# Graph network: the ranks of empty nodes and free slots move from the ordering stage into layer 0, with a weight split

## The reference

```python
edge_index = jnp.stack([src, dst])
h = jnp.maximum(_layernorm(x), 0.0)
x = x + _L0_gnn_ref(h, edge_index, L0_W1, L0_b1, L0_W2, L0_b2)
...
def gnn_layer(x, W, b, src, dst):          # _L0_gnn_ref: two of these
    h = x @ W.T + b
    agg = segment_sum(h[src], dst, num_segments=10000)
    return relu(agg)
```

## Time and profile before

| | us |
|---|---|
| median of 3 runs (2781.2 to 2782.97) | 2782.51 |
| the profiled execution | 2777.66 |
| its span in the profile | 2775.9 |
| Orders, from the first instruction after the barrier to that after the next | 290.0 to 342.9 |
| layer 0, first half | 342.9 to 668.8 |

### The profile page before, as it was taken

How to read it: one execution, slowest core, us unless ns; L and a number is a source line. 1 busy time by engine, 2 the same in 40 slices (tenths; PEclk the granted TensorE clock), 3 DMA queues, 4 the chain that set the end, 5 groups by cost and what they waited for, 6 DMA issues and landing times. The chain is left out here.

```text
span 2775.9 us, 48023 instructions
## 1 busy us (share of the span) xinstructions
PE 2503.1 (90%) x13886; PEld 2134.6 (77%) x13886; DVE 2015.0 (73%) x5259; ACT 1397.0 (50%) x2905; POOL 1739.8 (63%) x1849
## 2 busy tenths in 40 slices
PE   3666199998999969999999979999999699999998
PEld 3444088887888859999999868888888588888886
DVE  7888566664666637878788768888888566666666
ACT  0766054544888845555555434333333255555554
POOL 0777255554677776777777567777777455555554
PEclk9999999999999989999999989999999899999999
DMA  8888434333455543343333244333333255555553
GB/s 253 244 245 240 147 101 136 112 120 114 134 158 169 176 158 99 116 130 115 115 115 115 70 120 143 116 115 115 113 113 113 90 143 153 153 153 153 153 150 115
DMA packets 146046, 388.08 MB, mean 140 GB/s; under 512 B 34372, under 2 KB 34692, under 8 KB 145315
## 3 DMA queue, kind: packets, MB, share of 16 engines
q0 software_dynamic: 101408, 304.38, 37.0%
q1 hardware_dynamic: 43442, 80.04, 9.4%
q10 hardware_dynamic: 1056, 2.10, 0.2%
HBM read 261.83 MB, written 149.12 MB: 148 GB/s over the span
## 5 line engine op out<-in xcount | busy, mean ns | idle before, releaser
L1609 PE MATMUL c_pu<-c_Zhi,parts 128*128 128x256 f32 x640 | 182.1, 285 | 5.3 <-DVE c_Zlo L1527 5.3
L845 POOL DMA_INDIRECT f_Gsrc<-rows,indexS x80 | 80.5, 1006 | 168.6 <-PE f_phsrc L2110 159.7
L2026 ACT ACTIVATE f_Mhi<-f_pm 128x512 fp32r<-128x512 f32 x80 | 47.9, 599 | 266.1 <-DVE f_pm L2059 259.5
L1611 PE MATMUL c_pu<-c_Zhi,parts 128*128 128x256 f32 x640 | 181.6, 284 | 0.0
L1610 PE MATMUL c_pu<-c_Zlo,parts 128*128 128x256 f32 x640 | 180.5, 282 | 0.0
L2050 DVE TENSOR_TENSOR f_Hlosrc<-f_phsrc,f_Hhisrc 128x512 fp32r<-128x512 f32 x80 | 55.4, 692 | 158.6 <-ACT f_Hhisrc L2020 158.6
L1768 ACT CAST d_Hhi<-d_ph 128x512 fp32r<-128x512 f32 x80 | 46.8, 585 | 229.5 <-PE d_ph L1889 229.5
L849 POOL DMA_INDIRECT h<-a_rows,indexD x80 | 80.5, 1006 | 126.3 <-ACT a_rows L1184 119.7
L1496 ACT ACTIVATE c_pu<-c_pu,c_b1col 128x256 f32<-128x256 f32 x160 | 61.8, 450 | 162.6 <-PE c_pu L1611 162.6
L824 PE MATMUL b_po<-parts,b_Thi 128*128 128x512 f32 x320 | 132.6, 414 | 1.8 <-ACT b_po L1176 1.7
L824 PE MATMUL a_po<-parts,a_Thi 128*128 128x512 f32 x320 | 132.5, 414 | 0.4 <-DVE a_Tlo L1216 0.3
(11 more groups left out here) (461 smaller groups left out, 9623.0 us busy)
## 6 DMA issues: line engine op xcount, KB each, us to landing
rows<-r_xt SPq DMA_DIRECT2D x40, 520.0 KB, 4.0
h<-q_zerorow SPq DMA_DIRECT2D x80, 256.0 KB
r_xt<-in_x SPq DMA_DIRECT2D x80, 256.0 KB, 4.8
selrowsD<-selD SPq DMA_DIRECT2D x1, 2640.0 KB, 9.5
selrowsS<-selS SPq DMA_DIRECT2D x1, 2640.0 KB, 14.7
q_keyrowD<-in_dst POOLq DMA_DIRECT2D x1, 2560.0 KB, 17.7
q_keyrowS<-in_src POOLq DMA_DIRECT2D x1, 2560.0 KB
o_wstage<-in_L_W ACTq DMA_DIRECT2D x2, 1024.0 KB, 5.5
```

The source lines that it names most:

```text
L845: return pool.indirect_dma_start(out, None, table, bass.IndirectOffsetOnAxis(ap=rows, axis=0))
L1609: pe.matmul(psum_u[:, o, :], g.Whi[2][:, c, cols], Zhi[:, c, :], start=c == 0, stop=False)
L1611: ins = pe.matmul(psum_u[:, o, :], g.Wlo[2][:, c, cols], Zhi[:, c, :], start=False, stop=c == C - 1)
L2026: nc.scalar.activation(Mhi[s][:, :], psum_m[s][:, :], ACT.Relu).then_inc(s_Mhi, 1)
```

## The change

- Orders loads only one weight, `L0_W1`, on SP's queue and behind the wait for the records. ACT copies it in four quarters, and DVE instead of POOL subtracts, in four quarters, behind the step that makes `free`. `L0_W2` becomes the first of three weights that layer 0's first half loads and splits between its groups.
- SP writes `selrow` of D, waits for it, issues D's broadcast, and then does the same for S.
- The ranks leave Orders. That of empty nodes ("z") is worked out at the start of layer 0's first half, by PE and DVE before their loops; DVE's wait for the bias row stands behind it. That of free slots ("q") is cut up: PE has a piece behind groups 0, 2 and 4, DVE behind groups 1, 3 and 5. SP stores `qhi16` behind the third weight's load and waits for it before it issues the broadcast of `qdram`.
- PE's and DVE's loops have 6 groups written out in place of 2; ACT's are all written out. Some tiles have other places in memory.

```diff
@@ Orders, DVE
-                for m, (rows, out_row, name) in enumerate(((empty, zrow, "z"), (free, qrow, "q"))):
...
-                step(dve.tensor_copy(qhi16[:, :], qi[:, :]), "qhi16")
+                for c in range(C):
+                    dve.wait_ge(o_high, c + 1)
+                    dve.tensor_tensor(g.Wlo[0][:, c, :], wstage[:, c, :], g.Whi[0][:, c, :].bitcast(F32), ALU.subtract)
@@ Orders, ACT
-                for m in range(2):
-                    W.load_one(act, m)
-                    W.split_high(act, m)
+                act.wait_ge(o_w, 16)
+                for c in range(C):
+                    nc.scalar.copy(g.Whi[0][:, c, :], wstage[:, c, :]).then_inc(o_high, 1)
@@ Orders, POOL
-                for m in range(2):
-                    W.split_low(pool, m)
@@ Orders, SP
                 for k in KEYS:
                     sp.wait_ge(o_ld[k], 48)
-                for m, k in enumerate(KEYS):
+                sp.dma_start(wstage[:, :, :], io.L0_W1.rearrange("(c p) n -> p c n", p=P)).then_inc(o_w, 16)
+                for k in KEYS:
                     sp.wait_ge(o_v, marks["sel" + k])
                     sp.dma_start(g.seldram[k], selrow[k][:, :]).then_inc(o_sel[k], 16)
-                for k in KEYS:
                     sp.wait_ge(o_sel[k], 16)
                     sp.dma_start(g.selrows[k][:, :, :], g.seldram[k].partition_broadcast(P)).then_inc(o_bc[k], 16)
...
-                sp.wait_ge(o_v, marks["qhi16"])
-                sp.dma_start(g.qdram, qhi16[:, :]).then_inc(o_q, 16)
-                sp.wait_ge(o_q, 3 * 16)
+                sp.wait_ge(o_q, 2 * 16)
@@ layer 0, first half
-        W = None if second else Weights(nc, e, g, [(2, io.L1_W1), (3, io.L1_W2)])
+        W = None if second else Weights(nc, e, g, [(1, io.L0_W2), (2, io.L1_W1), (3, io.L1_W2)])
@@ SP
                 W.load(sp)
+                sp.wait_ge(n_step, marks["qhi16"])
+                sp.dma_start(g.qdram, qhi16[:, :]).then_inc(n_q, 16)
+                sp.wait_ge(n_q, 16)
                 sp.dma_start(qrow16[:, :], g.qdram.rearrange("t j -> (t j)").partition_broadcast(NT)).then_inc(e_ld, 16)
@@ ACT
-                pipeline(act, GR, 1, 1, body, between=lambda i: W.high_part(act, i), first=2 * C + 2)
+                straight(GR, 1, 1, body, between=lambda i: W.high_part(act, i))
@@ DVE
+            def step_node(ins):
+                ins.then_inc(n_step, 1)
+                steps[0] += 1
+                dve.wait_ge(n_step, steps[0])
+            def count_nodes(name, rows, m):
+                dve.wait_ge(n_pe, 3 * m + 1)
+                step_node(dve.tensor_copy(colform[:, :], pflag[:, 0:NT]))
+                if name == "z":
+                    step_node(dve.tensor_copy(emptyc[:, :], colform[:, :]))
+                step_node(dve.tensor_reduce(total[:, :], rows[:, :], AX.X, ALU.add))
+                step_node(dve.tensor_scalar(totals[:, :], g.ones_f[0:NT, :], total[:, 0:1], None, ALU.mult))
+            def place_nodes(name, m):          # 1 step, after a wait for PE
...
+            def split_ranks(name, m):          # 8 steps for z, 10 for q, after a wait for PE
...
+            def rank_free(i):
+                if i == 1:
+                    count_nodes("q", g.free, 1)
+                elif i == 3:
+                    place_nodes("q", 1)
+                elif i == 5:
+                    split_ranks("q", 1)
...
-            if not second:
-                dve.wait_ge(s_brow, 16)
             dve.wait_ge(s_const, 4 if second else 3)
...
-                pipeline(dve, GR, 1, 1, body)
+                count_nodes("z", g.empty, 0)
+                place_nodes("z", 0)
+                split_ranks("z", 0)
+                dve.wait_ge(s_brow, 16)
+                pipeline(dve, GR, 1, 1, body, between=rank_free, first=6)
@@ PE
+            def flag_nodes(name, rows, m):
+                if m:
+                    pe.wait_ge(n_step, marks["colz"])
+                pe.transpose(pflag[:, 0:NT], rows[:, :], g.ident[0:NT, 0:NT]).then_inc(n_pe, 1)
+            def count_up(name):                # 2 products
...
+            def turn_places(name):             # 1 transpose
...
+            def rank_free(i):                  # i == 0: flag, 2: count_up, 4: turn_places, of "q"
...
-                pipeline(pe, GR, 1, 0, body)
+                flag_nodes("z", g.empty, 0)
+                count_up("z")
+                turn_places("z")
+                pipeline(pe, GR, 1, 0, body, between=rank_free, first=6)
```

More of the change, by code:

```diff
@@ L131, in prepare_orders @@
     g.xs = [nc.dram_tensor(f"rows{n}", [N + 1, EXT], F32, kind="Internal").ap() for n in range(1, 4)]
+    g.hold = ExitStack()
+    held = Env(nc, g.hold, "h_")
+    g.empty, g.free = g.listed, held.sb("free", [NT, P], F32)
+    g.before_f, g.ones_f = held.sb("beforef", [P, P], F32), held.sb("onesf", [P, P], F32)
+    before_f, ones_f, empty, free = g.before_f, g.ones_f, g.empty, g.free
     with ExitStack() as ctx:
@@ L534, in prepare_orders @@
         tmp_c2 = sb("tmpc2", [P, NT], F32)
[L535 to L543, removed]
         with ExitStack() as c4:
@@ L712, in _ @@
                     pe.transpose(ptr[k][:, 2 * NT:3 * NT], length[k][:, :], g.ident[0:NT, 0:NT]).then_inc(o_pe, 1)
[L713 to L720, removed]
-                    pe.wait_ge(o_v, marks["row" + name])
-                    pe.transpose(prank[:, 0:NT], out_row[:, :], g.ident[0:NT, 0:NT]).then_inc(o_pe, 1)
             @block.sync
@@ L1007, in layer0 @@
     if not second:
-        g.hold = ExitStack()
-        g.qrow16 = g.hold.enter_context(nc.sbuf_tensor("qrow16", [NT, N], I16))
+        g.hold2 = ExitStack()
+        g.qrow16 = g.hold2.enter_context(nc.sbuf_tensor("qrow16", [NT, N], I16))
     qrow16 = g.qrow16
@@ L1040, in layer0 @@
             e_made, e_put, e_ld = e.sem("e_made"), e.sem("e_put"), e.sem("e_ld")
+            colform, total, totals = e.sb("colform", [P, NT], F32), e.sb("total", [NT, 1], F32), e.sb("totals", [NT, P], F32)
+            place = {k: e.sb("place" + k, [NT, P], F32) for k in "zq"}
+            rank_c = {k: e.sb("rankc" + k, [P, NT], F32) for k in "zq"}
+            whole, part_i, emptyc = e.sb("whole", [P, NT], I32), e.sb("parti", [P, NT], I32), e.sb("emptyc", [P, NT], F32)
+            qi, qhi16 = e.sb("qi", [NT, P], I32), e.sb("qhi16", [NT, P], I16)
+            pflag, psum_r, prank = (e.ps(n, [P, 512]) for n in ("pflag", "psumr", "prank"))
+            n_step, n_pe, n_q = e.sem("n_step"), e.sem("n_pe"), e.sem("n_q")
+            marks = {}
         s_brow, s_const = e.sem("s_brow"), e.sem("s_const")
@@ L1052, in layer0 @@
         block = ctx.enter_context(e.block())
+        if not second:
+            marks.update({"totalsz": 4, "placez": 5, "colz": 6, "totalsq": 16, "placeq": 17, "colq": 18, "qhi16": 27})
         @block.sync
@@ L1335, in put @@
                           stop=isinstance(T.t, int) and T.t == NT - 1).then_inc(e_put, 1)
+            def flag_nodes(name, rows, m):
[3 more added lines that the diff above has]
+            def count_up(name):
+                pe.wait_ge(n_step, marks["totals" + name])
+                pe.matmul(psum_r[0:NT, 0:P], colform[:, :], g.before_f[:, :], start=True, stop=False)
+                pe.matmul(psum_r[0:NT, 0:P], g.before_f[0:NT, 0:NT], totals[:, :], start=False, stop=True).then_inc(n_pe, 1)
+            def turn_places(name):
+                pe.wait_ge(n_step, marks["place" + name])
+                pe.transpose(prank[:, 0:NT], place[name][:, :], g.ident[0:NT, 0:NT]).then_inc(n_pe, 1)
+            def rank_free(i):
+                if i == 0:
+                    flag_nodes("q", g.free, 1)
+                elif i == 2:
+                    count_up("q")
+                elif i == 4:
+                    turn_places("q")
             def look(T):
```

56 lines of the change are left out of this document (28 added, 28 removed).

## The result

The changed kernel takes 2758.61 us (median of 6, 2757.4 to 2760.57); beside it the kernel before took 2782.05 (6, 2778.46 to 2782.97). The ratio is 0.9921, interval 0.9911 to 0.9932: faster by 23.4 us, where 17.8 was forecast. The profiled execution took 2758.56, its span is 2756.8, only 19.1 less than the profiled one of before.

The account below looks back on a forecast made before the run. Orders was taken to be bound by DVE's chain, layer 0's first half by PE. Orders' gain of 19.5 less 0.9 for z and 0.8 for q gave 17.8 us, so a median of 2764.7, range 2760.5 to 2772.

Parts of the forecast that it names:

- its whole 8.38: Orders: two long DVE steps beside POOL's subtractions become short, taking 8.38 us off DVE's chain.
- the 11.24: Orders: the stretch from 328.90 to 340.14 goes when the ranks leave, 11.24 us.
- The tables: Rival in Orders: S's table lands 5.4 us late and bounds in DVE's place; gain 12.7, time 2769.8; chance 0.15.
- the late case: Orders: S's store gets through only after D's broadcast; S's broadcast issued about 310.3, landing 319.8, 1 us to spare.
- Records: Start of Orders: loads ahead of the weight land in 2.4 us, DVE starts at 293.2; gain 2.9 us.
- I put the balance at 0: Layer 0's first half: third weight's transfer and qrow cost nothing on balance; bounds a gain of 1.6, a loss of 3.3.
- the bound of -1.6: Layer 0's first half: possible gain of 1.6 us if the pause before qrow lets the gathers through.
- its slow rival: Layer 0's loop: TensorE's lower clock lasting through groups 0 to 4 adds 77 us, time 2842; chance 0.03.
- I carry that difference over: Whole kernel: the profiled execution's 4.85 us below the median is kept, so 2759.9 profiled becomes 2764.7 median.
- the one that gained more than forecast: Rival: records land at 1.4 us and qrow's stall is gone; gain 20.3, time 2762.2; chance 0.12.
- the thin columns: Rival at Orders' start: thin columns take 5.1 us anyway, records not faster; gain 14.9, time 2767.6; chance 0.15.
- a costlier layer 0: Rival in layer 0: q at 2.1 us on PE and two transfer bursts; gain 13.2, time 2769.3; chance 0.10.

Follow-up runs that it names:

- e1: Kernel before with only the weight part changed: one weight in Orders, its subtraction on DVE, order of loads and ranks as before; 2774.77 us against 2780.0.
- e2: Changed kernel with both weights split in Orders by POOL and the old order of loads and stores, so only the ranks move; 2770.95 us, ratio 0.997.
- u1: Changed kernel with ACT issuing the weight's load at its start, beside the records' loads instead of behind them; 2763.36 us, ratio 0.9942 to the kernel before.
- b0: Kernel before, unchanged, profiled once more; 2780.99 us against 2780.0, its profiled execution 2780.75.
- a1: Changed kernel, unchanged, run once more beside the kernel before on one chip; 2757.1 us against 2781.47.
- u2: Changed kernel with the store of qdram ahead of the third weight, so weight and qrow follow at once; 2762.08 us, its profiled execution 2756.37.
- u4: Changed kernel with qdram's store ahead of the third weight, no pause before qrow, run a second time; 2759.09 us, ratio 0.9928 to the kernel before.
- p1: Kernel before with one wait added, for the second weight to land, ahead of qrow; 2776.6 us against 2780.3.
- w2: Changed kernel with 12 unused identity products ahead of PE's loop in layer 0's second half and 8 ahead of its first multiplication; 2756.39 us.
- v1: Changed kernel with DVE's four subtractions moved from Orders to layer 0's first half, the staged weight sharing memory; 2753.4 us, ratio 0.9904 to the kernel before.
- w1: Changed kernel with 12 unused identity products ahead of PE's loop in layer 0's second half; 2757.26 us, ratio 0.9915 to the kernel before.
- u3: Changed kernel with SP's old order, both selrow stores ahead of both broadcasts; 2758.49 us, ratio 0.9925 to the kernel before.

## Why the prediction missed, step by step

**Right.** Orders is DVE's chain, and what left the chain left the time. POOL's overlap was worth its whole 8.38 (e1, e2). The ranks were worth 7.95 and the 3.05 us that e2 waits, 11.0 of the 11.24. Orders of e1 and e2 with the 3.47 of u1 and those 3.05 give 5.95 + 7.95 + 3.47 + 3.05 = 20.4, and 20.6 to 20.8 were measured. The tables did not bind: by the reading of the Trainium skill, DMA: Bandwidth & Descriptors, section Queues, rings and completion order, S's store would sit behind D's broadcast. The trace agrees: D's broadcast lands at 300.70 + 8.7 = 309.4, S's store after 4.4 us at 309.6. S's broadcast was issued at 309.62, where the late case said 310.3. The clock of the loop stayed 1.00, and its regular tile 3.87 although more groups are written out.

**Small errors in Orders.** Records 3.4 to 3.5, not 2.9 (1.9 us to land, not 2.4); the subtraction 2.50, not 2.76; the tables 0, not 0.3. Together they are about the 1.2 us by which Orders gained more than the forecast 19.5.

**The first failed step: "I put the balance at 0"**, the third weight and `qrow`. The half comes apart at PE's `a_plist` products. To the first of them it takes 12.55 and 12.78 us before (b0 second), 14.13 and 13.20 after (a1 second): z costs 1.0 on average, where 0.9 was forecast, although the first sum comes 1.30 later. The 79 tiles behind it take 307.62 and 307.73 before, 306.13 and 306.04 after. In them q costs 0.65 (tiles of 3.98, 4.31 and 3.98 us where its pieces stand, against 3.87), where 0.8 was forecast partly by luck: the row of 0.38 us is one product in two instructions, not two products, and q has six instructions at 0.11 us each. The late tile falls from 6.39 and 6.52 to 4.25 and 4.13, by 2.3. 1.0 + 0.65 - 2.3 is -0.6, and so it was: the half did not grow by 1.7, its means are 326.07 before and 325.46 after. The balance was a gain of 2.3, not 0. The mechanism stood in the prediction as the bound of -1.6 (the pause lets the gathers through), and the price was read off the wrong place: 1.63 us is PE's idle time in 4 us of the timeline, while a tile that is late by 2.5 shows what the stall costs. u2 and u4 bring 1.9 of the 2.3 back without the pause, and p1 takes the late tile out of the kernel before. The other 0.4 is that the tile without a pause takes 5.90 and 6.25 in u2 and u4, not 6.4 to 6.5; why, the runs don't show.

**The start of that half, which the prediction read past.** The first `a_plist` product scatters between executions of one kernel by up to 0.9 us, and TensorE's clock goes with it. PE's instructions on 128x512 there, in the changed kernel:

```profile
334.68 0.63 PE L784 MATMUL a_po<-parts,a_Thi 128*128 128x512 f32 x1
335.40 0.39 PE L786 MATMUL a_po<-parts,a_Tlo 128*128 128x512 f32 x1
```

In layer 0's second half such an instruction takes 0.63 us at a granted clock of 0.50 and 0.39 at 1.00, so the lower level lasts here until about 335.2, 12.3 us into the half; in a1 0.39 stands already 10.7 us in, in p1 9.3. The column of the granted clock reads 1.00 throughout, as it does in Orders, so ahead of its first change it doesn't show the level. The prediction argued against its slow rival that the loop starts behind an emptier stretch and is granted 1.00: at the start it wasn't, in either kernel. That the later groups ran at 1.00, before and after, stands.

**The second failed step: "I carry that difference over"**, the 4.85 us between the profiled execution and the median. That difference was no constant of the program: the profiled execution of after lies at its median. Each execution has its mean granted clock beside its time. Of the kernel before these are the 47 that ran beside the experiments, b0's own not counted:

| granted clock | before: executions, mean us | changed, with a1: executions, mean us |
|---|---|---|
| 0.981 | 21, 2781.57 | none |
| 0.982 | 5, 2780.90 | 6, 2758.87 |
| 0.983 | 17, 2778.00 | 4, 2757.13 |
| 0.984 | 4, 2776.79 | 1, 2757.40 |

The profiled execution of before, 2777.66, has 0.983, while most executions have less; that of after has 0.982 and lies at its median. At equal clock the change is worth 22.0, 20.9 and (by one execution) 19.4 us; the spans of the two profiled executions each differ by 20.6 on average. The other 2 to 3 us of the 23.4 go with the kernel before running at 0.981 in 21 of 47 executions (b0 in 6 of 11), and the changed one in none of 11. That the clock makes those 2 to 3 us isn't shown, and the mean clock is a rough label: at 0.983 the kernel before takes 2775.32 to 2780.00, and at 0.982 one and the same program takes 2762.35 on average as u2 and 2759.09 as u4. Besides, the first comparison's 2782.05 is high for the kernel before: beside the experiments its medians were 2780.0, 2780.3 and 2781.47. The prediction for the profiled execution, 2759.9, was 1.3 off; the 4.85 added to it put the forecast of the median 6.1 too high.

**Between the two steps**: 17.8 forecast, 1.2 more in Orders and 2.3 more in the first half give 21.3, within what equal clocks show. The 2.1 us from there to 23.4 stand in no stage. Of the rivals the one that gained more than forecast, 20.3 with quick records and `qrow`'s stall gone, named the right two terms; I gave it 0.12. The tables, the thin columns and a costlier layer 0 are refuted by the changed kernel's waits, u1 and the stage table; the clock in the loop by its 1.00.

**What stays open.** Why the kernel before falls to 0.981 so often. b0's longer execution places 2.3 of 3.1 us in layer 0's second half, whose clock came up 7 us later, and in w2, with the clock up earlier, that half is 1.6 to 1.8 shorter. Against the full story: e1 has 0.981 in 7 of 11 executions, p1 in none of 11, though its clock in the profiled one came up only 13.4 us into the second half. By these two the pause at `qrow` seems to matter here too, but u2 and u4, without it, have 0.981 in none of 10. Also open are the longer executions of u2 and the pace of v1's tiles.

## What to carry to other kernels

Read a stall's price from the distance between repeats of the loop where it stands, not from the bound engine's idle time in a window around it. Before a profiled execution is tied to a median, look where it lies among the other executions, by time and by granted clock: the difference is not a constant that another kernel inherits. And let thin loads that start a chain go ahead of a large one, and keep two large transfers apart where gathers must get through.

## What the runs showed of the hardware

- The same code in the same stage, layer 0's second half, is granted the full clock at different times: for good from 8.2 us (u2), 8.8 (before), 12.6 (a1) or 15.8 (b0) into it, with 345.15, 345.76, 346.60 and 348.08 us for the half. In the changed kernel and in w1 it rose at 7.2 and 3.3 us and fell again at 10.6 and 10.1, after PE had stood still for 2.0 and 1.8 us; in before it did not fall, with PE still for 1.6.
- Two large loads of SP's queue in a row (1 MB and 1.6 MB) delay one of POOL's gathers so that a tile takes 5.9 to 6.5 us instead of 3.87 (before, b0, e1, u2, u4); a store of 20 KB between them, 5.4 us from issue to landing, brings it to 4.1 to 4.7 (the changed kernel, a1, u1, u3, w1, w2), a wait for the landing to 3.87 (p1).
- 0.3 KB of thin columns land in 1.9 us without the 1 MB load of another queue and in 5.1 to 5.2 beside it (before, u1). A 20 KB store lands in 1.4 us alone and in 4.4 to 4.6 behind a 2.6 MB broadcast of its own queue (the changed kernel, u1).
- In v1 the one POOL descriptor step that began beside one of DVE's subtractions took 1.31 us, with 0.94 to 1.00 for its neighbours and at most 1.01 for this gather's steps in every other run. It is a single observation, and its cause isn't shown:

```profile
321.89 0.69 DVE L1283 TENSOR_TENSOR parts<-h_scratch,parts 128x512 fp32r<-128x512 f32 x1
322.11 1.31 POOL L805 DMA_INDIRECT a_G<-rows,indexD  x1 [0.30 <-issue]
323.72 0.95 POOL L805 DMA_INDIRECT a_G<-rows,indexD  x1 [0.30 <-issue]
```
